# The second group's scatter, taken apart and put between the answers of the first group

## The chip, the cores and the metric

The kernel runs on one core of a Trainium2 chip. The metric is device time in microseconds from the start to the end of one execution. The profile is that of one further execution; its span runs from the first to the last instruction and is a little shorter than the execution's own time.

## What is computed

One decoder layer in float32 on x of shape (32, 128, 128): self-attention with 16 heads, cross-attention with 16 heads over 4 key/value heads, and a mixture of 8 experts of which each token gets 2. Each of the three ends in a residual and a layer norm. The change touches only the third part:

```python
scores = (jnp.einsum('btd,ed->bte', x, router_w) + router_b) / temp
gates = _sinkhorn(scores)                       # 3 iterations
topk_vals, topk_idx = jax.lax.top_k(gates, K)   # K = 2 of E = 8
topk_gates = topk_vals / (jnp.sum(topk_vals, axis=-1, keepdims=True) + 1e-08)
g = jax.nn.relu(jnp.einsum('btd,edf->btef', x, wg))
p = jnp.einsum('btd,edf->btef', x, wp)
all_out = jnp.einsum('btef,efd->bted', g * p, wo)
...
x = _layernorm(x + x + expert_out)
```

## The kernel before, in words

**Sparse experts.** The reference computes all eight experts for each token; the kernel computes the two that are chosen. The 32 batches are split into two groups, `plan = Sparse([20, 12])`: group 0 has 20 batches, group 1 has 12. In a group, each of the 128 tokens of each batch is written twice, once for each of its experts, to rows of a DRAM tensor `placed[g]` that is ordered by expert and padded to blocks of 128 rows. A group of n batches has 2n + 7 blocks: 47 blocks in group 0 and 31 in group 1, in all NB = 78.

**Dispatch.** `pool_dispatch` (lines 1340 to 1349) does that writing. For each batch b and each of the two experts it issues one indirect DMA from GpSimd (POOL), which scatters 128 rows of 132 floats of `x2_all` to the rows that `place[g]` names. For group 1 that is 12 x 2 = 24 indirect DMAs. With `first == 0` it waits beforehand for the cleared buffer and for the routing step SLOT, which yields the places.

**Loads.** SyncE (lines 1474 to 1480) loads the blocks back into SBUF in chunks of up to eight. Ahead of the first chunk of group 1 it waits for `scattered[1]`, that is for all 24 dispatches of the group.

**The block loop.** TensorE, ScalarE and VectorE each run their steps in an order written out by block number i, from 0 to 77. On TensorE, iteration i has the transpose of block i + 1 (line 1665), the two up projections of block i as three matmuls (1672 to 1674), the transposes of the hidden values of block i - 1 (1680) and the down projection of block i - 2 (1687). ScalarE makes `x_hi` (1532), the relu `gs` (1537) and `hT` (1542); VectorE makes `x_lo` (1597), the product `h` (1603), and the weighted answer `ysb[:, i, :]` (1609). `ysb` has a place for each of the 78 blocks, so nothing waits for an answer to leave SBUF. The routing of group 1 (softmax iterations, top-2, places) runs in small steps beside the blocks of group 0; its SLOT step stands in iteration 24 and its table of owners in iteration 25.

**Sends.** GpSimd runs `send(i)` (lines 1514 to 1520) for each block in order: it waits for answer i (`y_done`), and issues one indirect DMA that scatters the 128 answers back to token order in `answered[g]`. Each counts up `y_sent[g]`. In front of `send(24)` (`DISPATCHED = 24`) GpSimd issues all 24 dispatches of group 1.

**The end.** The 8 quads of four batches are gathered by SyncE (`take`, line 1487), which waits until all sends of the quad's group are there: 47 for group 0, 31 for group 1. Quads 0 to 3 are added and normalised beside blocks 60 on (`JOINED`; line 1614 is the first step), the others after the last block; line 1554 normalises, line 1493 stores.

Of the kernel before, what the change touches and what calls it, by code (L numbers as in the profile page):

```python
# [1367 lines left out]
def ffn_phase(nc, sem, ps, routing, plan, x2_all, fw_hi, fw_lo, fwo_sb, ident, mhalf, eps, f_lo, fo_loaded, xg_first, first_loaded, placed, answered,  # L1368
# [7 lines left out]
    with ExitStack() as phase:  # L1376
# [72 lines left out]
        DISPATCHED = 24  # L1449
# [22 lines left out]
        @block.sync  # L1472
        def _(sp):
            for n, (g, c0, c1) in enumerate(chunks):
                if n == 0:
                    continue
                if g and c0 == 0:
                    sp.wait_ge(scattered[g], 16 * 2 * plan.size[g])
                sp.dma_start(rows(g, c0, c1), placed[g][c0 * 128:c1 * 128, :].rearrange("(n p) d -> p n d", p=128))\
                    .then_inc(xg_loaded[n], 16)  # L1480

            def take(q):
                g, b = plan.quads[q]
                row = (b - plan.first[g]) * 2 * S
                sp.wait_ge(y_sent[g], 16 * plan.blocks[g])
                wait(sp, acc_step, 2 * (q - QB + 1))
                sp.dma_start(yq[q % QB][:], answered[g][row:row + FB * 2 * S, :].rearrange("(b s k) d -> s b (k d)", s=S, k=2))\
                    .then_inc(yq_loaded[q % QB], 16)

            def give(q):  # L1490
                sp.wait_ge(yo_ready, FB * (q + 1))
                b = plan.quads[q][1]
                sp.dma_start(out[b:b + FB, :, :].rearrange("a s d -> s a d"), yo[q % QB][:]).then_inc(stored[q % QB], 16)

            for q in range(len(JOINED)):
                take(q)
            for q in range(len(JOINED), len(plan.quads)):
                if plan.quads[q][0] == 0:
                    give(q - QB)
                    take(q)  # L1500
            for q in range(len(plan.quads) - QB):
                if plan.quads[q + QB][0]:
                    give(q)
            for q in range(len(JOINED), len(plan.quads)):
                if plan.quads[q][0]:
                    take(q)
            for q in range(len(plan.quads) - QB, len(plan.quads)):
                give(q)
            for p in range(QB):
                sp.wait_ge(stored[p], 16 * quads_before(p, len(plan.quads)))  # L1510

        @block.gpsimd
        def _(pool):
            def send(i):
                g = plan.group_of[i]
                j = i - plan.block0[g]
                pool.wait_ge(y_done, i + 1)
                nc.gpsimd.indirect_dma_start(  # L1518
                    answered[g], bass.IndirectOffsetOnAxis(goes_to[g][:, j:j + 1], 0), ysb[:, i, :], None,
                    bounds_check=plan.size[g] * 2 * S + plan.blocks[g] * 128 - 1, oob_is_err=False).then_inc(y_sent[g], 16)  # L1520

            for i in range(NB):
                if i == DISPATCHED:
                    routing.pool_dispatch(pool, 1, placed[1], 0, plan.size[1], cleared, scattered[1])
                send(i)

        @block.scalar
# [236 lines left out]
```

## Time and profile before

| | us |
|---|---|
| median of 3 runs | 970.75 |
| lowest and highest | 966.46, 970.96 |
| the profiled execution | 968.17 |
| its span | 966.4 |
| TensorE busy in the span | 869.0 (90%) |
| VectorE, ScalarE, GpSimd busy | 723.9, 702.5, 558.2 |
| TensorE's mean granted clock | 0.968 |

The attention part ends and the block loop starts near 785 us; the last block's answer is written near 944 us. A line of a timeline has the start in us, the duration in us, the engine, the line of the code, the operation, out<-in, the count, and in brackets how long the engine was idle before it and what ended that. "issue" is time in which the engine waited for nothing that the profile shows.

### The profile page before, as it was taken

Reading aid. Unit: us, or ns where it says so; the run is one execution under the profiler, and the core shown is the slowest. Engines: PE = TensorE matmul, PEld = TensorE weight load, DVE = VectorE, ACT = ScalarE, POOL = GpSimd, SP = SyncE. Lnnn points to the kernel's source line nnn. Section 1 sums busy time; section 2 is a strip of 40 time slices with the busy share of each in tenths; the row PEclk is TensorE's granted clock in tenths of the full one; section 3 lists DMA queues with packets and bytes.
Section 4 is the critical chain, followed back from the end, with each engine's and each line's share of the span. In section 5 each row is a group of like instructions: output and inputs, shape, how many; then the busy total and the mean of one; then the engine's idle time right before and its main releaser. Section 6 shows DMA issues by size and latency. Waiting matters only on the chain. (4 is left out here: it accounts for less than half of the span.)

```text
span 966.4 us, 23079 instructions
## 1 busy us (share of the span) xinstructions
PE 869.0 (90%) x6694; PEld 675.3 (70%) x6694; DVE 723.9 (75%) x2124; ACT 702.5 (73%) x2471; POOL 558.2 (58%) x846
## 2 busy tenths in 40 slices
PE   4999999999999999999999988699999659998990
PEld 2677777777777777777777766577777537776770
DVE  3478888888888888888888787888888736754674
ACT  3688878888888888888888887478888526454564
POOL 5565555555555555555555554388788404577761
PEclk9999999999999999999999999899999979999995
DMA  4991000000000000000000000001000051114434
GB/s 127 254 100 26 10 9 8 8 8 8 8 8 11 8 8 8 11 11 8 8 10 10 10 9 10 1 29 32 26 24 21 24 134 35 34 55 140 140 99 131
DMA packets 63299, 39.17 MB, mean 41 GB/s; under 512 B 15904, under 2 KB 60192, under 8 KB 63232
## 3 DMA queue, kind: packets, MB, share of 16 engines
q1 hardware_dynamic: 58688, 28.89, 13.2%
q0 software_dynamic: 4544, 9.45, 2.9%
q8 instruction: 35, 0.57, 0.3%
q14 instruction: 32, 0.26, 0.1%
HBM read 21.51 MB, written 16.81 MB: 40 GB/s over the span
## 5 line engine op out<-in xcount | busy, mean ns | idle before, releaser
L465 ACT ACTIVATE prob<-ps,negmax 128x128 f32<-128x128 f32 x512 | 181.8, 413 | 10.2 <-DVE negmax L584 10.2
L385 POOL TENSOR_TENSOR prob<-prob,recip 128x512 f32<-128x512 f32 x128 | 136.9, 1079 | 43.1 <-DVE recip L589 43.0
L473 ACT ACTIVATE xprob<-ps,xmax 128x128 f32<-128x128 f32 x512 | 145.3, 423 | 19.7 <-DVE xmax L584 19.7
L394 POOL TENSOR_TENSOR qk_sin<-qk,sin_sb 128x128 f32<-128x128 f32 x256 | 115.7, 473 | 59.2 <-ACT qk L452 58.8
L465 ACT ACTIVATION_READ_ACCUMULATOR prob<-ps,negmax 128x1 f32 x512 | 129.9, 254 | 0.0
L584 DVE TENSOR_REDUCE xmax<-ps 128x4 f32<-128x512 f32 x128 | 87.3, 689 | 32.7 <-PE ps L873 32.1
L1518 POOL DMA_INDIRECT answered<-ysb,goes_to x78 | 77.0, 987 | 56.9 <-DVE ysb L1609 40.8
L452 ACT ACTIVATE qk<-ps 128x512 f32<-128x512 f32 x128 | 74.2, 606 | 49.1 <-PE ps L790 49.0
L400 POOL TENSOR_TENSOR qk<-qk_cos,qk_sin 128x256 f32<-128x256 f32 x128 | 94.7, 741 | 20.1 <-DVE qk_cos L593 20.1
L409 POOL TENSOR_TENSOR ve<-mv,eps 128x1 f32<-128x1 f32 x64 | 12.2, 191 | 155.1 <-DVE mv L607 154.7
L584 DVE TENSOR_REDUCE negmax<-ps 128x4 f32<-128x512 f32 x128 | 84.9, 685 | 17.8 <-PE ps L814 17.7
L788 PE MATMUL ps<-w_lo,xT_hi 128*128 128x512 f32 x192 | 91.4, 476 | 7.4 <-DVE xT_lo L618 7.4
L760 PE MATMUL ps<-ident,prob 128*128 128x128 f32 x512 | 79.0, 277 | 10.6 <-POOL prob L385 9.4
L814 PEld LDWEIGHTS ps<-kT,qT 64*128 64x128 f32 x1024 | 64.6, 194 | 28.3 <-issue 28.3
L760 PE MATMUL ps<-ident,qk 128*128 128x128 f32 x512 | 75.5, 281 | 3.6 <-POOL qk L400 3.6
L760 PEld LDWEIGHTS ps<-ident,prob 128*128 128x128 f32 x512 | 60.3, 141 | 24.6 <-POOL prob L385 9.1
L814 PE MATMUL ps<-kT,qT 64*128 64x128 f32 x1024 | 77.1, 292 | 0.0
L790 PE MATMUL ps<-w_hi,xT_hi 128*128 128x512 f32 x192 | 76.9, 401 | 0.0
L789 PE MATMUL ps<-w_hi,xT_lo 128*128 128x512 f32 x192 | 76.6, 399 | 0.0
L1347 POOL DMA_INDIRECT placed<-x_all,place x64 | 63.6, 993 | 18.3 <-issue 17.7
L760 PE MATMUL ps<-ident,xprob 128*128 128x128 f32 x512 | 72.4, 280 | 0.0
L834 PE MATMUL ps<-probT,v 128*64 128x128 f32 x1024 | 70.0, 279 | 0.0
(211 smaller groups left out, 2238.3 us busy)
## 6 DMA issues: line engine op xcount, KB each, us to landing
xg<-placed SPq DMA_DIRECT2D x8, 528.0 KB, 7.0
yq<-answered SPq DMA_DIRECT2D x8, 512.0 KB, 5.5
placed<-blank_x SPq DMA_DIRECT2D x1, 3008.0 KB, 26.9
xf<-in_x SPq DMA_DIRECT2D x32, 64.0 KB, 1.9
xres<-in_x SPq DMA_DIRECT2D x32, 64.0 KB
cx<-in_ctx SPq DMA_DIRECT2D x32, 64.0 KB, 1.8
out_y<-yo SPq DMA_DIRECT2D x8, 256.0 KB, 2.3
placed<-blank_x SPq DMA_DIRECT2D x1, 1984.0 KB, 24.9
```

Of the source, the lines that this page charges most:

```text
L385: nc.gpsimd.tensor_tensor(prob[:, n], prob[:, n], recip[:, n, :, None].broadcast_to([128, 4, S]), ALU.mult).then_inc(normed, 1)
L394: last = nc.gpsimd.tensor_tensor(sines[:, :, side, :], part[:, :, 1 - side, :], table, ALU.mult)
L400: nc.gpsimd.tensor_tensor(qk[:, 8 * n:8 * n + 8, 0:ROPE], qk_cos[:, 8 * n:8 * n + 8, :], qk_sin[:, 8 * n:8 * n + 8, :], ALU.add).then_inc( ...
L465: last = nc.scalar.activation(prob[:, n, j, :], bank(name)[:, j * S:(j + 1) * S], ACT.Exp, bias=negmax[:, n, j:j + 1], accum_out=sums[:, n ...
L473: last = nc.scalar.activation(xprob[:, n, g, :], bank(name)[:, g * S:(g + 1) * S], ACT.Exp, bias=xmax[:, n, g:g + 1])
L584: nc.vector.tensor_reduce(dst, bank(name).rearrange("p (j s) -> p j s", j=4), AX_X, ALU.max, negate=True).then_inc(done, 1)
L760: return nc.tensor.transpose(dst, src, ident[:])
L788: nc.tensor.matmul(dst, xT_hi[:], w_lo[:, cols], start=True, stop=False)
L789: nc.tensor.matmul(dst, xT_lo[:], w_hi[:, cols], start=False, stop=False)
L790: done(f"f.Q{n}", nc.tensor.matmul(dst, xT_hi[:], w_hi[:, cols], start=False, stop=True))
L814: last = nc.tensor.matmul(dst[r][:, j * S:(j + 1) * S], qT[q][rows, 4 * u + j, :], kT[q][rows, 4 * u + j, :], start=False, stop=(j == 3), ...
L1518: nc.gpsimd.indirect_dma_start(answered[g], bass.IndirectOffsetOnAxis(goes_to[g][:, j:j + 1], 0), ysb[:, i, :], None, bounds_check=plan.si ...
```

## The change

In front of `send(24)` the group's 24 dispatches stood in one row. Now two of them, those of batch b = i - 24, stand in front of each of the sends 24 to 35. The arguments of `pool_dispatch` are `b, b + 1` in place of `0, plan.size[1]`, so its wait stands ahead of b = 0 alone, as before. The number of DMAs and their contents stay as they are.

```diff
             for i in range(NB):
-                if i == DISPATCHED:
-                    routing.pool_dispatch(pool, 1, placed[1], 0, plan.size[1], cleared, scattered[1])
+                b = i - DISPATCHED
+                if 0 <= b < plan.size[1]:
+                    routing.pool_dispatch(pool, 1, placed[1], b, b + 1, cleared, scattered[1])
                 send(i)
```

## Rows read from the trace of the kernel before

**Rows 1.** The chain that ended last, 855 to 890 us: start, us, what.
```profile
860.93 0.97 POOL placed L1347
...
872.43 2.45 DMA placed<-x_all,place
874.90 5.14 DMA xg<-placed
880.09 0.33 PE ps L1665
```

**Rows 2.** The table of waits from 780 us: who, for whom, total us, times, longest.
```profile
PE ps L1665 <- DMA xg<-placed: 3.3, 1, 3.3
```

**Rows 3.** TensorE's timeline where the chain leaves it.
```profile
876.14 0.61 PE L1687 MATMUL ps<-fwo_sb,hT 128*128 x4
880.09 0.33 PE L1665 MATMUL ps<-ident,xg 128*128 128x128 f32 x1 [3.34 <-DMA xg<-placed]
```

**Rows 4.** GpSimd's timeline: first and last dispatch, sends behind them, and the end.
```profile
843.03 0.97 POOL L1347 DMA_INDIRECT placed<-x_all,place  x1 [0.30 <-issue]
...
872.43 0.97 POOL L1347 DMA_INDIRECT placed<-x_all,place  x1 [0.30 <-issue]
873.71 0.97 POOL L1518 DMA_INDIRECT answered<-ysb,goes_to  x1 [0.30 <-issue]
...
901.84 0.97 POOL L1518 DMA_INDIRECT answered<-ysb,goes_to  x1 [0.30 <-issue]
...
935.07 0.97 POOL L1518 DMA_INDIRECT answered<-ysb,goes_to  x1 [0.95 <-DVE ysb L1609]
...
945.22 1.40 POOL L1518 DMA_INDIRECT answered<-ysb,goes_to  x1 [0.37 <-issue]
```

**Rows 5.** Lines 1347 and 1518 by themselves: ns min/median/max, first and last start.
```profile
L1347 POOL DMA_INDIRECT placed<-x_all,place x64: 969/974/1213, 628.8 to 872.4; - x64
L1518 POOL DMA_INDIRECT answered<-ysb,goes_to x78: 967/973/1398, 795.5 to 945.2; - x78
```

**Rows 6.** VectorE's timeline: answers 24 and 46, the first add, answer 77.
```profile
842.49 0.34 DVE L1609 TENSOR_SCALAR ysb<-ps,weight 128x128 f32<-128x128 f32 x1
...
887.07 0.35 DVE L1609 TENSOR_SCALAR ysb<-ps,weight 128x128 f32<-128x128 f32 x1 [0.41 <-PE ps L1687]
...
909.23 0.68 DVE L1614 TENSOR_TENSOR acc<-yq 128x512 f32<-128x512 f32 x1
...
944.09 0.35 DVE L1609 TENSOR_SCALAR ysb<-ps,weight 128x128 f32<-128x128 f32 x1 [0.99 <-PE ps L1687]
```

**Rows 7.** The DMA queue of SyncE, 872 to 905 us.
```profile
874.90 5.09 SPq L1479 DMA_DIRECT2D xg<-placed  x4
904.10 0.95 SPq L1487 DMA_DIRECT2D yq<-answered  x2
```

**Rows 8.** The chain that ended last, its end.
```profile
945.22 2.67 DMA answered<-ysb,goes_to
947.90 3.94 DMA yq<-answered
```

**Rows 9.** Windows: busy us (x instructions) by engine, then granted clock, DMA share, GB/s.
```profile
788.00:790.00 2.00, 2.00 (x6) 1.56 (x7) 0.29 (x1) 0.56 (x2) 0.00 (x0) 0.50 1.12 330
...
876.80:880.00 3.20, 0.00 (x0) 0.00 (x0) 0.42 (x2) 0.00 (x0) 2.38 (x3) 1.00 1.06 311
880.00:881.00 1.00, 0.91 (x4) 0.76 (x5) 0.24 (x1) 0.28 (x1) 0.90 (x1) 0.92 1.12 340
881.00:882.00 1.00, 1.00 (x6) 0.80 (x5) 0.11 (x2) 0.43 (x2) 0.69 (x2) 0.50 1.15 328
...
884.00:885.00 1.00, 1.00 (x9) 0.94 (x8) 0.28 (x1) 0.66 (x2) 0.91 (x1) 0.88 0.40 129
```

**Rows 10.** Line 1603 in 800 to 841 and in 843 to 876 us: ns min/median/max.
```profile
L1603 DVE TENSOR_TENSOR h<-ps,gs x20: 412/424/426, 801.7 to 840.3; 128x256 f32<-128x256 f32 x20
L1603 DVE TENSOR_TENSOR h<-ps,gs x18: 424/425/425, 844.0 to 874.7; 128x256 f32<-128x256 f32 x18
```

## The prediction

> **What bounds the kernel now.** I read four views, in this order: the chain that ended last, the table of waits, the timelines of GpSimd, TensorE, VectorE and the DMA queue around the point where the chain leaves TensorE, and the table of windows with the granted clock.
>
> The chain [rows 1] shows whether GpSimd is ever on the path. From 860.93 us on it is: nine dispatches of line 1347 run head to tail, the tenth of that stretch is the last of the 24 (start 872.43), it lands 2.45 us later, the load of the second group's first rows (line 1479) lands 5.14 us after that, and at 880.09 TensorE transposes them (line 1665). The wait table [rows 2] gives the same point from TensorE's side: one wait of 3.3 us on xg<-placed. So the second group's 24 dispatches are not hidden. They are the reason that TensorE stands idle from 876.75 (876.14 + 0.61) to 880.09 [rows 3]. Their cover is the first group's remaining blocks, which end at 876.75, and that cover is already short by 3.34 us. Whatever makes the last dispatch later now makes TensorE later by the same amount.
>
> **What the edit moves.** No instruction is added or removed: 24 dispatches, 78 sends, the same waits. Only GpSimd's order changes. Before, at i = 24, it issues dispatches 1 to 24 and then sends 24 to 46. After, it issues two dispatches, send 24, two dispatches, send 25, and so on to i = 35. The wait for the places (SLOT) and for the cleared buffer stands at b = 0 in both, so the first dispatch keeps its start, 843.03.
>
> **Price of one send in that queue.** In the timeline of GpSimd [rows 4] a dispatch is busy for 0.97 and another 0.30 passes before the next. From start to start it is (872.43 - 843.03) / 23 = 1.278 over the burst. Sends behind the burst keep the same distance: 22 steps from 873.71 to 901.84, 1.279 each. The medians of the two kinds are 974 and 973 ns [rows 5]. So one send in front of a dispatch delays it by 1.279 us. Bounds: 0.97 if the 0.30 gap vanished when kinds alternate, 1.7 if every one were as long as the longest send (1.398 + 0.30). I take 1.279, since the same gap stands where the two kinds already meet (872.43 to 873.71).
>
> **How many stand in front.** The last dispatch (i = 35) gets sends 24 to 34 ahead of it: 11 of them, 11 x 1.279 = 14.07 us. Its start moves from 872.43 to 886.50. With the bounds above: 10.7 to 18.7 us.
>
> For this price the Trainium skill has a figure of its own: DMA: Bandwidth & Descriptors, section Specifications, gives about 1 us to the first byte of a DMA issued through GpSimd. With that as the whole price of a send the shift would be an estimate of 11 us. The trace's 1.279 us from start to start is longer, since it has the gap between two in it, and the sum goes by the trace.
>
> **Do the sends add waiting of their own?** send(i) waits for answer i, and dispatches are now queued behind that wait, with SyncE's load behind them. Answer 24 is written at 842.49 + 0.34 = 842.83 [rows 6]; a waiting send starts some 0.78 us behind its answer (945.22 behind 944.44 [rows 4, 6]), so send 24 could start at 843.61. It would start at 843.03 + 2 x 1.279 = 845.59, send 25 at 849.43. A block takes (874.7 - 844.0) / 17 = 1.81 us [rows 10], three DMAs of GpSimd take 3.84, so the answers only run further ahead. Cost of these waits: 0; the distance is smallest at send 24, 2 us.
>
> **What follows from the last dispatch.** Landing 2.45 and load 5.14 are unchanged: before, too, sends followed directly behind the last dispatch, and the same four loads of the second group are issued together [rows 7]. TensorE resumes at 880.09 + 14.07 = 894.16. It stands idle from 876.75, thus 17.4 us instead of 3.3. The transpose that waits is that of block 47, which stands in iteration 46 ahead of the products of block 46, so answers 44, 45 and 46 wait too, and with them VectorE and ScalarE; nothing else is ready for any of the three, because their order is written out by block.
>
> **Is anything given back?** First, sends 24 to 34 leave earlier. Nobody reads the answers one by one: SyncE's take(0) waits for all 47 sends of the first group. These and the 24 dispatches are 47 DMAs on GpSimd in either order, so send 46 would again start at 901.84 if its answer is there. Answer 46 comes at 887.07 + 0.35 + 14.07 = 901.49, so that send starts at about 902.3, and take(0) goes out at about 904.6 instead of 904.10 [rows 4, 6, 7]. Its rows are first needed at iteration 60 (line 1614), before at 909.23 [rows 6], then at 923.3. That is no stall. Second, GpSimd has a backlog now: from 843 on it first waits for an answer at 935.07 [rows 4]. After, answers 47 on arrive 14 us later and GpSimd follows them one by one. The backlog was off the path either way: the end of the chain [rows 8] is the last send at 945.22, which starts 0.78 us behind its answer, its landing, the last quads' load and their normalisation. All of this hangs on block 77 of TensorE, and moves by the whole 14.07.
>
> **The clock.** In the windows [rows 9] the granted clock is 1.00 while TensorE idles from 876.8 to 880, 0.92 in the first microsecond of work, 0.50 (the 1.2 GHz level) from 881 to 884, 0.88 in the next, then 1.00 (2.4 GHz). So the 3.3 us pause already costs some 3.7 us at the lower level. Near the start of the block loop, after loose work, the window 788 to 790 is at 0.50 as well. After a pause of 17.4 us the clock should be low from the first matmul on: 0.9 us more at half speed, at most 0.45 us lost, and if the low stretch is then counted from the restart it ends up to 0.7 us earlier. I take +0.2 us, with -0.4 to +1.9 as bounds (the latter if the low stretch is 3.8 us longer, half of it lost).
>
> Beside this the Trainium skill, TensorE: Matmul & The Clock Gate, section HAM oscillation, says that a long wait for a DMA makes the next stretch start cold. The trace agrees for the short pause, and by the rule alone, one cold start here and one there, the clock's part would be 0.
>
> **Sum.** 14.07 + 0.2 = 14.3 us. Against the profiled execution: 968.17 us, of which the span is 966.4, becomes 982.5 (span 980.7). The three runs have a median of 970.75, 2.6 above the profiled one, and a lowest of 966.46; with 14.3 they give 985.1 and 980.8. I say 984.5, between 982.5 and the median's 985.1 but nearer the latter, because two of the three runs lie at 971.
>
> **Rivals.**
> (a) Not slower: the backlog takes it up. If the end were set by the number of DMAs that GpSimd has to issue, their order would not matter, and the time would stay at 968 to 971. For it: GpSimd waits for no answer from 843 to 934. Against it: with every answer ready, the last send would start at 901.84 + 31 x 1.279 = 941.5, and it starts at 945.22; with the shift it starts at 959.3. The backlog would decide only if a send took (959.3 - 901.84) / 31 = 1.85 us, against 1.279 measured. A dense GpSimd that slows the others is no source of a gain either: line 1603 takes 425 ns in the dense stretch and 424 in the loose one [rows 10]. Chance 0.04.
> (b) Slower still: the restart is worse than it is now, with the clock low for twice as long or sends above 1.28 us as they alternate with dispatches of another destination. +1.9 us by the clock's bound, up to +4.6 us by the longest send, gives 986.4 to 989.1. For it: single DMAs of 1.21 and 1.40 us exist. Against: the medians are within 6 ns of the shortest [rows 5]. Chance 0.09.
> (c) A smaller loss: the gap between two shrinks or TensorE's restart is better than now. 0.97 x 11 = 10.7 us, 3.4 below the 14.07, gives 979.1 to 981.7. Against: the gap was 0.30 at both kinds and at their border. Chance 0.05.
> (d) The edit does not act as said, for instance because the dispatches start late. The condition 0 <= b < 12 gives exactly i = 24 to 35, and answer 24 is early by 2 us; I give this 0.01, either way.
> The forecast itself, full shift on the path, has 0.81.
>
> **How the numbers follow.** Range: the low end takes in the lowest run with the full shift (980.8) and touches (c); the high end 988 takes in the highest run (970.96 + 14.3 = 985.3), the clock's bound and the lower half of (b). A measurement of this kernel can tell about 0.5%, 4.85 us, from no change. Every case but (a) and part of (d) is 10 us or more slower: slower 0.95, within 0.5% 0.04, faster 0.01.
>
> **What would show it.** In GpSimd's timeline: first dispatch near 843.0, two dispatches and a send in turn, last dispatch near 886.5. In the waits: TensorE on xg<-placed once for about 17.4 us, ending near 894.2. The clock at 0.50 directly after it. take(0) near 904.6, and line 1614 not waiting for it. The last send near 959.5, following its answer; GpSimd waiting for answers from about send 46 on. Wrong would be: a DMA distance other than 1.28 (the price), a wait shorter than the last dispatch's delay asks for (the chain), or a block distance below 1.8 us in the second group that earns the delay back.

## The result, and the profile after

| | before | after |
|---|---|---|
| median, us | 970.75 (4 runs) | 984.75 (4 runs) |
| lowest and highest | 966.46, 970.96 | 983.66, 986.31 |
| the profiled execution | 968.17 | 986.31 |
| its span | 966.4 | 984.5 |
| TensorE's mean granted clock | 0.968 | 0.949 |

The change costs 14.0 us: the ratio is 1.0156, 95% interval 1.0124 to 1.0188, that is 12.0 to 18.3 us. The forecast was 984.5 us, from 14.07 us of queueing and 0.2 us of clock.

These four runs of each kernel are the first set. Three more sets were run for the experiments, each on one chip: number 11 in the second, 12 in the third, and 11 again in the fourth, half an hour after the second; the first set's chip is not on record. The kernel before took 1007.5 and 1005.3 us in the second and third set, and 969.9 us in the fourth (medians of 29 runs each). This is no scatter: the lowest of the 29 runs lies above 1002 in the second and third, the highest below 975 in the fourth. Nor is it a property of the chip, since by the record number 11 gave both 1007.5 and 969.9. So every comparison below is made within one set, and what makes some 36 us of difference between the sets is a finding of its own further down.

First the chain that ended last, of the changed kernel (start, us, what):

```profile
887.34 0.97 POOL placed L1347
888.31 0.30 issue
888.62 0.97 POOL answered L1518
889.59 0.30 issue
889.89 0.97 POOL placed L1347
890.87 0.31 issue
891.17 2.45 DMA placed<-x_all,place
893.63 4.25 DMA xg<-placed
897.92 0.48 PE ps L1666
```

Where [rows 1] had dispatches alone, a send now stands after every second dispatch, in the chain itself: that is the price, in sight. Line numbers behind 1525 are one higher than before, so L1666 is the transpose L1665 of [rows 2, 3]. The timeline of GpSimd, first and last dispatch and what stands beside them:

```profile
847.77 0.97 POOL L1347 DMA_INDIRECT placed<-x_all,place  x1 [0.30 <-DVE ysb L1610]
849.05 0.97 POOL L1347 DMA_INDIRECT placed<-x_all,place  x1 [0.30 <-issue]
850.33 0.97 POOL L1518 DMA_INDIRECT answered<-ysb,goes_to  x1 [0.30 <-issue]
851.60 0.97 POOL L1347 DMA_INDIRECT placed<-x_all,place  x1 [0.30 <-issue]
...
891.17 0.97 POOL L1347 DMA_INDIRECT placed<-x_all,place  x1 [0.31 <-issue]
892.45 0.97 POOL L1518 DMA_INDIRECT answered<-ysb,goes_to  x1 [0.30 <-issue]
...
906.50 0.97 POOL L1518 DMA_INDIRECT answered<-ysb,goes_to  x1 [0.31 <-issue]
908.34 0.97 POOL L1518 DMA_INDIRECT answered<-ysb,goes_to  x1 [0.87 <-DVE ysb L1610]
```

From the first dispatch to the last are 43.40 us, 29.40 in [rows 4]: 14.00 us more, 1.273 for each of the 11 sends. The distance stays at 1.28 where the kinds meet. TensorE's side, from its timeline and the table of waits:

```profile
880.91 0.61 PE L1688 MATMUL ps<-fwo_sb,hT 128*128 x4
897.92 0.48 PE L1666 MATMUL ps<-ident,xg 128*128 128x128 f32 x1 [16.40 <-DMA xg<-placed]
```

```profile
PE ps L1666 <- DMA xg<-placed: 16.4, 1, 16.4
```

One wait, as in [rows 2], now 16.4 us instead of 3.3. The clock, from the table of windows (columns as in [rows 9]):

```profile
897.00:898.00 1.00, 0.08 (x1) 0.08 (x1) 0.00 (x0) 0.00 (x0) 0.69 (x2) 0.50 1.14 355
898.00:899.00 1.00, 1.00 (x3) 0.89 (x4) 0.25 (x1) 0.28 (x1) 0.70 (x2) 0.50 1.16 349
899.00:900.00 1.00, 1.00 (x5) 0.70 (x5) 0.04 (x1) 0.20 (x1) 0.81 (x1) 0.50 1.11 323
900.00:902.00 2.00, 2.00 (x9) 1.83 (x9) 1.07 (x3) 0.85 (x3) 1.59 (x2) 0.54 1.16 322
```

The clock is at its lower level (1.2 GHz) from the first matmul on. It was low already before that, in the idle window 894 to 895. From TensorE's resumption to the first up projection of block 49 it takes 905.48 - 897.92 = 7.56 us; before it took 887.45 - 880.09 = 7.36.

The two profiles laid side by side, each part by its own start and end in the two traces:

| part | before | after | difference | forecast |
|---|---|---|---|---|
| up to the first dispatch | 843.03 | 847.77 | +4.74 | 0 |
| first dispatch to last | 29.40 | 43.40 | +14.00 | +14.07 |
| last dispatch to TensorE's transpose | 7.66 | 6.75 | -0.91 | 0 |
| from there to block 49 | 7.36 | 7.56 | +0.20 | +0.2 |
| from there to the end | 78.95 | 79.02 | +0.07 | 0 |

The span differs by 18.1 us, of which 4.74 lie ahead of the first line that the change touches. The start of that part moves from one execution to the next in every kernel here (the first dispatch lay between 843.0 and 847.8 in the profiles of the first and fourth set), and the profiled execution is also the longest of the four. The local difference, 13.4 us, is the one to hold against the 14.0 of the medians.

That the median came out within 0.3 us of the forecast is in part luck: the runs of the kernel before are spread over 4.5 us, and one term of the sum was off by 0.9 us (see below). That it was measured in a set like the first at all was luck too, as the second set shows.

### The profile page after: what moved, and what is told of

Read it like the earlier page. It is cut to its first block and busy times, and to the rows that moved or that the text cites. A ratio compares the mean times of both kernels' runs of the same rounds, so it can differ in the third digit from the quotient of the medians.

```text
span 984.5 us, 23047 instructions
## 1 busy us (share of the span) xinstructions
PE 876.1 (89%) x6662; PEld 680.9 (69%) x6694; DVE 724.4 (74%) x2124; ACT 701.5 (71%) x2471; POOL 556.4 (57%) x846
## 5 line engine op out<-in xcount | busy, mean ns | idle before, releaser
L409 POOL TENSOR_TENSOR ve<-mv,eps 128x1 f32<-128x1 f32 x64 | 12.1, 189 | 159.6 <-DVE mv L607 159.2
L760 PEld LDWEIGHTS ps<-ident,prob 128*128 128x128 f32 x512 | 60.2, 141 | 24.3 <-POOL prob L385 8.9
L1347 POOL DMA_INDIRECT placed<-x_all,place x64 | 63.5, 992 | 18.3 <-issue 17.7
```

Of the source, the lines that this page charges most:

```text
L760: return nc.tensor.transpose(dst, src, ident[:])
```

## The experiments

The theory: the change costs as many GpSimd DMAs as it puts ahead of the last dispatch, 1.28 us each, because TensorE waits for the load behind that dispatch. The rivals: interleaving costs as such; the backlog absorbs; or the loss is another.

### Second set: both kernels again, and two other numbers of sends

The kernel before, once more, unchanged:

> The kernel before, once more, for a second profile. Both theories: the 24 dispatches start near 843 to 848 us and are 29.4 us from the first start to the last. It tells two things apart. If the start near 843 belongs to the kernel before, it is 843 again; if the attention part ahead of it differs from one execution to the next, it lies anywhere from 841 to 848, and TensorE's wait is 3 to 4 us all the same. If the load of 5.14 us (issue to TensorE's transpose) belongs to a row of dispatches without sends between them, it is 5.1 again; if it varies by execution it is anywhere from 4.2 to 5.2.

Measured: ratio 0.9998 (0.9981 to 1.0016) to the kernel before of its set, at 1007.4 us. The dispatches took 29.4 us in a row as always, but from 853.7 to 883.1, and TensorE did not wait for the load at all. No theory had that. The rows are below.

The changed kernel, unchanged:

> The changed kernel, once more. Theory (11 sends of 1.28 us stand ahead of the last dispatch): 43.4 us from the first dispatch to the last plus one step, TensorE waits 16 to 17.5 us, ratio to the kernel before 1.0145 (14.0 us), within 1.012 to 1.017. Rival (the profiled 18 us of difference belong to the change): ratio 1.0185.

Measured: 1.0008 (0.9995 to 1.0021). All numbers of the expectation are missed. In this set the change costs nothing that can be measured. The dispatches took 49.5 us from first to last here, since sends 27 and 31 each waited 3.3 us for their answers. TensorE waited for the load not at all.

Four dispatches in front of each of six answers:

```diff
-                b = i - DISPATCHED
+                b = 2 * (i - DISPATCHED)
                 if 0 <= b < plan.size[1]:
-                    routing.pool_dispatch(pool, 1, placed[1], b, b + 1, cleared, scattered[1])
+                    routing.pool_dispatch(pool, 1, placed[1], b, b + 2, cleared, scattered[1])
```

> The 24 dispatches go four at a time in front of six answers, so 5 sends stand ahead of the last one instead of 11. Theory: last dispatch later than in the kernel before by 5 x 1.278 = 6.4 us, TensorE waits 3.3 + 6.4 = 9.7 us, time 6.4 to 6.8 us above the kernel before, ratio 1.0068. Rival (interleaving as such costs, whatever the number, by alternating two destinations): close to the changed kernel, ratio 1.013 or more. Rival (a backlog of GpSimd absorbs): ratio 1.000.

Measured: 1.0006 (0.9991 to 1.0020). The theory's 1.0068 is missed. It is what the absorbing rival gives, but for another reason than a backlog of GpSimd.

Twelve pairs spread over answers 24 to 43:

```diff
-                b = i - DISPATCHED
-                if 0 <= b < plan.size[1]:
-                    routing.pool_dispatch(pool, 1, placed[1], b, b + 1, cleared, scattered[1])
+                for b in range(plan.size[1]):
+                    if i == DISPATCHED + 19 * b // 11:
+                        routing.pool_dispatch(pool, 1, placed[1], b, b + 1, cleared, scattered[1])
```

> The twelve pairs of dispatches stand in front of twelve answers that are spread from 24 to 43, so 19 sends stand ahead of the last one. Theory: every send is ready when GpSimd comes to it, the last dispatch is 19 x 1.278 = 24.3 us later than in the kernel before, TensorE waits 27.6 us, time 24.3 us above, ratio 1.025. Rival (sends wait for their answers as well): more than 24.3, up to 30. Rival (the delay is partly taken up by the end, where GpSimd has no backlog any more): below 20.

Measured: 1.0062 (1.0041 to 1.0083), 6 us where 24.3 were expected. Here TensorE waits again, but 9.1 us and not 27.6:

```profile
926.81 0.47 PE L1666 MATMUL ps<-ident,xg 128*128 128x128 f32 x1 [9.10 <-DMA xg<-placed]
```

What is different in this set is seen in the windows of the kernel before (run before_again), around its dispatches:

```profile
843.00:853.00 10.00, 9.35 (x52) 7.00 (x51) 8.82 (x38) 4.93 (x16) 4.95 (x6) 1.00 0.10 33
853.00:893.00 40.00, 12.19 (x44) 7.84 (x44) 4.01 (x12) 3.50 (x11) 27.66 (x29) 0.59 0.31 91
893.00:903.00 10.00, 8.84 (x46) 7.36 (x47) 5.82 (x20) 5.25 (x17) 4.26 (x5) 0.78 0.24 69
```

TensorE is busy for 12 of 40 us, VectorE for 4, ScalarE for 3.5, while GpSimd issues its DMAs as fast as ever. By the answers (line 1609), blocks 24 to 28 take 40.4 us; in the first set they took 7.05. Who waits for whom is seen in the timelines of TensorE and ScalarE ("remote" is a wait for whose end the profile names no instruction):

```profile
856.91 0.30 PE L1665 MATMUL ps<-ident,xg 128*128 128x128 f32 x1 [0.33 <-issue]
...
857.69 0.40 PE L1674 MATMUL ps<-fw_lo,x_hi 128*128 x1
...
867.52 0.45 PE L1665 MATMUL ps<-ident,xg 128*128 128x128 f32 x1 [1.07 <-issue]
```

```profile
858.92 0.38 ACT L1537 ACTIVATE gs<-ps 128x256 f32<-128x256 f32 x1 [2.63 <-PE ps L1674]
...
866.77 0.28 ACT L1532 ACTIVATE x_hi<-ps 128x128 fp32r<-128x128 f32 x1 [5.32 <-remote]
...
872.42 0.38 ACT L1537 ACTIVATE gs<-ps 128x256 f32<-128x256 f32 x1 [5.37 <-remote]
```

The transpose of 856.91 ends at 857.21, and ScalarE's `x_hi`, which waits for it alone, starts 9.6 us later; in the last 5.3 of them ScalarE is idle. VectorE shows the same: the answer that waits for a down projection that ended about 856.6 is made at 864.63. The other way it is quick: x_lo is written by VectorE at 867.37, and TensorE transposes at 867.52. So while the dispatches run, what TensorE signals reaches the others late; every block needs several such signals. I call this the hold. By the trace it is the signal that is late, and not TensorE's work: the up projection behind that transpose ended at 858.09, and ScalarE's relu started on it at 858.92, so a later signal overtook an earlier one. The trace's own record of semaphore updates agrees: the update by the transpose stands at 866.75, the one by the up projection at 858.90. The hold outlasts the dispatches: the last one starts at 883.11, and the step from answer 27 to 28 ends at 893.60.

One more thing sets these traces apart. The six traces of the first and fourth set record 9996 to 10024 semaphore updates each, the eight of the second and third 8322 to 8481, and the missing ones all lie behind 620 us, where the first group's dispatches begin. Whether the loss of records and the hold have one cause, and whether the recording itself has a part in it, no run shows.

### Third set: what the dispatches cost here

All 24 dispatches of the second group left out; its load waits for the cleared buffer instead, and its quads read the first group's answers:

```diff
-                    sp.wait_ge(scattered[g], 16 * 2 * plan.size[g])
+                    sp.wait_ge(cleared, 16 * 2 * plan.groups)
...
-                if i == DISPATCHED:
-                    routing.pool_dispatch(pool, 1, placed[1], 0, plan.size[1], cleared, scattered[1])
                 send(i)
```

> The second group's 24 dispatches are left out: its blocks compute on blank rows, its answers go to the spare rows, and its quads read the first group's answers, so 12 of the 32 batches come out other than the reference's. Sends, loads and all block work stay. Theory A (dispatches cost only by being late): TensorE's wait of 3.3 us and the low clock behind it go, 3.3 to 5 us less than the kernel before, on any chip. Theory B (on some chips each dispatch also holds back the signals that TensorE gives the other engines, 1.4 us each, as blocks 24 to 44 of the last runs suggest): 3.3 to 5 us less where the kernel before takes 971, and 30 to 36 us less where it takes 1007.

Measured: 0.9676 (0.9655 to 0.9698), 972.5 us against 1005.3: 32.7 us less, as theory B said. Its windows:

```profile
843.00:853.00 10.00, 9.36 (x52) 7.08 (x51) 8.62 (x37) 4.68 (x15) 4.84 (x5) 1.00 0.10 33
853.00:893.00 40.00, 39.39 (x221) 30.26 (x220) 22.88 (x78) 20.59 (x66) 21.34 (x22) 1.00 0.11 38
```

TensorE is busy for 39.4 of the same 40 us. The hold goes with the dispatches. GpSimd still sends in that window, but only at the pace of the answers, so a rival stays: that any 24 DMAs head to tail would do it. The 33 us are not the whole difference between the sets either. Without the 24 dispatches there is no wait for them (3.3 us, and the low clock behind it), and still this run takes 972.5 us, more than the 970 of the kernel before in the other sets. The rest lies ahead of the block loop: the first group's 40 dispatches take 149.9 us from first to last here (627.4 to 777.3), 149.6 to 151.3 in the seven other traces of the second and third set, and 141.6 to 144.0 in the six of the first and fourth. Whether these 6 to 10 us are the same hold is not shown.

The dispatches in one row, but in front of send 30:

```diff
-        DISPATCHED = 24
+        DISPATCHED = 30
```

> The 24 dispatches in one row in front of send 30 instead of 24. Here six sends stand ahead, and GpSimd has to wait for the answers too. Where the kernel before takes 971: answer 29 is written at 852.3, send 29 starts near 853.1, the first dispatch near 854.4 instead of 843.0, so TensorE's load comes 11.3 us later, ratio 1.0117. Counting sends alone (6 x 1.278 = 7.7) gives 1.0079. Where it takes 1007: whether the hold of the blocks moves with the dispatches (blocks 24 to 29 then run at 1.8 us and 30 on are held) or stays where it is; time within 5 us of the kernel before.

Measured: 1.0012 (0.9995 to 1.0029). VectorE's timeline of answers 31 to 34:

```profile
861.89 0.34 DVE L1609 TENSOR_SCALAR ysb<-ps,weight 128x128 f32<-128x128 f32 x1
...
867.38 0.35 DVE L1609 TENSOR_SCALAR ysb<-ps,weight 128x128 f32<-128x128 f32 x1 [3.48 <-remote]
...
881.43 0.35 DVE L1609 TENSOR_SCALAR ysb<-ps,weight 128x128 f32<-128x128 f32 x1 [7.56 <-remote]
...
900.35 0.35 DVE L1609 TENSOR_SCALAR ysb<-ps,weight 128x128 f32<-128x128 f32 x1 [8.29 <-remote]
```

Blocks 24 to 31 run at their usual distances, 32 to 34 take 38.5 us. The hold moved with the dispatches, which began at 860.79.

Four dispatches in front of each of six answers, again:

> Four dispatches in front of each of six answers, once more. Where the kernel before takes 971 and TensorE waits for the load: 5 x 1.278 = 6.4 us above it, ratio 1.0066, TensorE's wait 9.7 us. Where it takes 1007 and the cover is 33 us longer: ratio 1.000 again. The rival that alternating two destinations costs as such: 1.013 in the first case.

Measured: 0.9991 (0.9975 to 1.0007): the case with the hold. So the steps between 0 and 11 sends ahead of the last dispatch were never measured without it.

The row in front of send 22, and the routing steps behind COUNT one block earlier:

```diff
-            ROUTED.setdefault(k - SINK * SINKHORN_ITERS // 2 + (1 if k > COUNT else 0), []).append((1, k))
+            ROUTED.setdefault(k - SINK * SINKHORN_ITERS // 2, []).append((1, k))
-        DISPATCHED = 24
+        DISPATCHED = 22
```

> The kernel before, with the second group's 24 dispatches in one row in front of send 22 instead of 24, and the four last routing steps of that group (ENDS to TABLE) one block earlier, so that the places are known one block earlier. Where the kernel before takes 971: the first dispatch starts 4 us earlier, TensorE's wait of 3.3 us on the load goes and the clock stays up, so 3.3 to 5 us less, 966 to 967.5, ratio 0.995 to 0.9965. Rival: sends 22 and 23 and the steps moved up collide with VectorE's other work beside the same blocks, gain 0 to 1. Where it takes 1007 and the block loop is held back anyway: ratio 1.000.

Measured: 1.0005 (0.9992 to 1.0018), as expected with the hold. This was meant as the version that beats both kernels. Whether it gains 3 to 5 us where nothing is held was not seen: it did not run in such a set.

Across these sets the hold is nearly the same whatever the arrangement. From answer 24 to answer 43, 34.4 us in the first trace of before, the held traces take 68.2 (one row), 68.6 (two at a time), 68.3 (four at a time), and 65.4 us (spread over 19, where it reaches past block 43), and no24, in such a set too but without the dispatches, 34.5. That is some 34 us for 24 dispatches, 1.4 each.

And it explains why the change cost nothing there. The 34 us are cover. In the row the load is issued at 885.42 and TensorE comes to its transpose at 921.26, where [rows 7, 3] had 874.90 and 876.75. After the change the load is issued at 904.46, still ahead of TensorE. Spread over 19 answers it is issued at 922.05, TensorE gets its rows at 926.81 after a wait of 9.1 us, and 6 us of time are lost. What holds in all three is the forecast's chain, last dispatch, load, TensorE, with another cover. Its count of 1.28 us a send does not: from first dispatch to last are 49.5 and 66.8 us, not 43.4 and 53.7, because the held answers keep the sends waiting.

### Fourth set: stand-ins for the dispatches

To have the order without the hold, 24 stand-ins took the place of the dispatches. They are sends in all but their destination:

```diff
+            def stand_in(j):
+                if j == 0:
+                    pool.wait_ge(cleared, 16 * 2 * plan.groups)
+                    pool.wait_ge(routing.by_dve, routing.dve_done(1, SLOT))
+                nc.gpsimd.indirect_dma_start(
+                    plan.spare, bass.IndirectOffsetOnAxis(goes_to[0][:, j:j + 1], 0), ysb[:, j, :], None,
+                    bounds_check=plan.size[0] * 2 * S + plan.blocks[0] * 128 - 1, oob_is_err=False).then_inc(scattered[1], 16)
...
-                    routing.pool_dispatch(pool, 1, placed[1], 0, plan.size[1], cleared, scattered[1])
+                    for j in range(2 * plan.size[1]):
+                        stand_in(j)
```

> In place of the second group's 24 dispatches GpSimd issues 24 stand-ins that are sends in all but their destination: the answers of blocks 0 to 23, 512 bytes a row, go to a spare tensor. They count up the same semaphore, so the load of the second group still waits for the last of them. The second group computes on blank rows and its quads read the first group's answers: 12 of 32 batches come out other than the reference's. Theory (sends do not hold back TensorE's signals, dispatches do): where the kernel before takes 1005, no block takes over 6 us but the one that waits for the load, the time is that of the kernel without dispatches (972) plus TensorE's wait of 3 to 4 us and the low clock behind it, 975 to 978, ratio 0.971. Rival (any 24 indirect DMAs in a row hold back the blocks): 1005, ratio 1.000.

Measured: 0.9996 (0.9979 to 1.0013), 970.65 us. In this set, on chip 11 like the second, the kernel before itself took 969.9, so it had no hold that the stand-ins could have avoided. The expectation's 0.971 is missed for that reason, and the question that it was to answer stays open. What it shows is that 24 plain sends in the dispatches' place cost the same as the dispatches.

The same stand-ins, two in front of each of twelve answers:

```diff
-                    for j in range(2 * plan.size[1]):
-                        stand_in(j)
+                    stand_in(2 * b)
+                    stand_in(2 * b + 1)
```

> The same 24 stand-ins, two in front of each of twelve answers, as the change has the dispatches. Theory (the change costs 11 sends of 1.278 us, as soon as nothing holds the blocks back): 14.1 us above the run with the stand-ins in one row, 989 to 992 where that has 975 to 978; TensorE waits 17 us. Rival (the loss on the first chip was something else than the number of sends in front of the last dispatch): within 5 us of it.

Measured: 1.0119 (1.0095 to 1.0143), 982.73 us: 12.1 us above the row of stand-ins. The expectation was 14.1. It is a second measurement of the change's price, on 12 and 6 runs, with other data in other places. The rival, within 5 us, is out. TensorE's transpose behind the load, first in the row, then in the mixed order:

```profile
882.10 0.48 PE L1675 MATMUL ps<-ident,xg 128*128 128x128 f32 x1 [4.12 <-DMA xg<-placed]
```

```profile
895.67 0.47 PE L1676 MATMUL ps<-ident,xg 128*128 128x128 f32 x1 [16.21 <-DMA xg<-placed]
```

The load is issued 31.64 us behind the first stand-in in the row (844.20 to 875.84), 45.65 in the mixed order (845.71 to 891.36): 14.01 us, the same as with the dispatches. The rest of the difference is the load itself: 6.26 us until the transpose in the row, 4.31 mixed.

Stand-ins in a row with the dispatches' source and row length, and with that source alone (there the edit takes the first 128 of the 132 floats, `0:D`):

```diff
-                    plan.spare, bass.IndirectOffsetOnAxis(goes_to[0][:, j:j + 1], 0), ysb[:, j, :], None,
+                    plan.spare, bass.IndirectOffsetOnAxis(goes_to[0][:, j:j + 1], 0), x2_all[:, plan.first[1] + j // 2, :], None,
```

> The 24 stand-ins in one row, but with the dispatches' source and row length: 132 floats (528 bytes) of x2_all to a spare tensor with rows of 528 bytes, at the places of the first group's answers. If the length of the row or its source is what holds the blocks back: 24 x 1.4 = 33 us above the stand-ins of 512 bytes, 1005 to 1010. If it is the dispatches' list of places or their destination: as the stand-ins of 512 bytes, 975 to 978.

> The 24 stand-ins in one row, with 128 floats (512 bytes) of x2_all as source and a spare tensor with rows of 512 bytes. If the source x2_all holds the blocks back: 1005 to 1010. If the row length of 528 bytes does: as the first stand-ins, 975 to 978.

Measured: 0.9985 (0.9968 to 1.0002) and 0.9984 (0.9967 to 1.0002). Neither tells anything about the hold, since the set had none. Both say once more that a GpSimd scatter costs the same in this queue whether its rows have 512 or 528 bytes.

## Why the prediction was right, step by step

- **The chain** (dispatch, landing, load, transpose) is confirmed by the chain of the changed kernel and its one wait of 16.4 us.
- **The price of a send**, 1.279 us, measured 14.00 / 11 = 1.273. The reason for taking the value between 0.97 and 1.7, that the 0.30 gap stood where the kinds meet, was sound.
- **How many stand in front**, 11: counted in the timeline.
- **No waiting of their own**: true in the first set, where GpSimd waits for no answer from the first dispatch to send 46 and first waits for that of block 47 (908.34; the forecast said about send 46). With the hold it is false, 49.5 us instead of 43.4 from first to last, and costs nothing there.
- **Landing and load unchanged**: the one term of the sum that was mis-sized. Together they are 6.75 us instead of 7.66, -0.91. With the rows of the six traces without the hold, the time from the load's issue to the transpose is 4.29 (after), 4.31 and 4.24 in three, and 5.19 (before), 6.26 and 6.29 in the other three. The latter are those in which the DMA table of just that stretch also shows a packet of the queue that the profile calls instruction, q8. For the kernel before, 875 to 881 us:

```profile
q8 instruction: 1, 0.02, 1.1%
```

  In the three short ones that queue has no packet between the issue and the transpose; in spread19, where TensorE waits for the load too, it has none either, and the time is 4.76. That this packet delays the load is argued from this, not shown by an experiment. Had the load taken equally long in both profiles, the table's local difference would be 14.3 us and not 13.4.
- **Nothing given back**: take(0) went out at 908.75, where the forecast's 904.6 and the 4.74 us of the earlier part give 909.3; the last send started at 963.42, where 959.3 and 4.74 give 964.0. The end behind block 49 differs by 0.07 us.
- **The clock**: +0.20 between the two profiles, +0.2 forecast. The low stretch of before adds up to 3.4 us by the windows of [rows 9] (0.16 + 3.0 + 0.24, from the shares 0.92, 0.50 and 0.88), not to the forecast's 3.7. By the rule of the Trainium skill (TensorE: Matmul & The Clock Gate, HAM oscillation) that a long wait for a DMA makes the next stretch start cold, the part would have been 0; the trace agrees with the cold start (0.50 from 897.92 on), and going cold 0.9 us earlier cost 0.2.
- **The price by the Trainium skill** (DMA: Bandwidth & Descriptors, Specifications), about 1 us to the first byte, would have given 11 us as an estimate; the trace has 14.00.
- **Rival (a)**, that something absorbs the delay, had 0.04 with GpSimd's backlog as its mechanism, and that mechanism is refuted: in the first and fourth set all of the delay of the load reaches the end. But its outcome is real in the second set, by a mechanism that no row of the first trace shows. The forecast was right for a state like that of the trace it was made from; it said nothing of how much of it depends on the cover of -3.3 us in that trace.

## What to carry to other kernels

Taking a burst apart makes nothing cheaper where the consumer waits for its last piece: in an in-order queue each foreign item put in between delays that last piece by one item. Count the items ahead of the last one, multiply by the distance from start to start (not by the busy time), and hold the sum against the cover that is left: here 11 x 1.28 us against -3.3 us. And a cover of a few us may belong to the moment as much as to the kernel: with the hold it was some 30 us, and on the chip that the record calls 11 the hold was there in one set and gone in the next. Measure both kernels side by side, and once more at another time, before the verdict is carried on.

## What was not expected of the hardware

- **The hold.** In two of four sets, while GpSimd issues the 24 dispatches (132 floats a row, scattered to DRAM), ScalarE and VectorE wait up to 9.7 us for signals of TensorE whose work had ended before, TensorE's clock falls to its lower level (0.50), and the block loop loses 33 to 34 us. It is there in all 29 runs of the kernel before in these sets and absent in the other two, of which the fourth has the same chip number as the second. Without the 24 dispatches it is absent in such a set as well, though GpSimd sends there at the pace of the answers. What does it is open: the row length, source, list of places or destination of a dispatch, or any row of GpSimd DMAs head to tail; and so is what differs between the sets. The runs meant to tell were made in a set without it.
- **The distance of GpSimd's indirect DMAs** is 1.28 us from start to start, in any mixture, at 512 and at 528 bytes a row, in all four sets.
- **The load's time** until TensorE can start is 4.2 to 4.8 us, or 5.2 to 6.3 in the three traces with a packet of the instruction queue in the same stretch.
